# Four inverse square roots per token group: from ScalarE's Ln and Exp to a VectorE-only chain

## The reference

```
x = x + attention(layernorm(x));   x = x + fp8_gemm(bf16(layernorm(x)), kernel) + bias
layernorm(x) = (x - mean) / sqrt(var + 1e-5)
attention: q, k, v = x @ W.T, 16 heads of 16 features, each mapped by
    exp_map(v) = 1/sqrt(c) * tanh(sqrt(c) * |v|) * v/|v|
  dist = 1/sqrt(c) * arccosh(max(1 + 2c * |q-k|^2 / ((1 - c|q|^2)(1 - c|k|^2)), 1 + 1e-5))
  weights = softmax(-softplus(beta) * dist - bias)
  out = log_map(exp_map(weights @ log_map(exp_map(v)))) @ W_o.T
```

## Time and profile before

| what | us |
|---|---|
| median of 3 runs (2428.98 to 2432.98) | 2432.06 |
| the profiled execution's own time | 2433.24 |
| span of its trace | 2431.4 |
| ACT busy (80% of the span) | 1937.7 |
| PE busy (80%) | 1945.1 |
| DVE busy (40%) | 970.8 |
| POOL busy (15%) | 362.6 |
| mean granted TensorE clock, share of full | 0.809 |

### The profile page before, as it was taken

One profiled execution on the slowest core, in us unless ns is written; L12 is line 12 of the kernel. 1 busy time (PEld: TensorE's weight loads), 2 busy tenths in 40 slices (PEclk: granted clock), 3 DMA queues, 4 the chain that ended last, 5 costly groups with the idle time before them and its releaser, 6 DMA issues. The chain is left out here.

```text
span 2431.4 us, 29241 instructions
## 1 busy us (share of the span) xinstructions
PE 1945.1 (80%) x10317; PEld 624.6 (26%) x10317; DVE 970.8 (40%) x2289; ACT 1937.7 (80%) x1184; POOL 362.6 (15%) x223
## 2 busy tenths in 40 slices
PE   4458897989888768888879489798979888888682
PEld 2222232323222222222323123232323222222221
DVE  4432344343534345343444534443343534221413
ACT  1039999998989659998989389899988989999491
POOL 1111121121212002020212102121121212010011
PEclk9959798988888778897989579898888888876675
DMA  1120101001010200202020020201001010200000
GB/s 37 57 57 10 49 10 51 25 19 58 18 58 1 66 9 11 65 1 75 1 66 10 1 75 1 66 10 66 10 18 58 18 49 1 66 1 18 1 18 10
DMA packets 79154, 75.58 MB, mean 31 GB/s; under 512 B 34651, under 2 KB 60508, under 8 KB 78940
## 3 DMA queue, kind: packets, MB, share of 16 engines
q1 hardware_dynamic: 78940, 73.02, 9.6%
HBM read 17.96 MB, written 55.05 MB: 30 GB/s over the span
## 5 line engine op out<-in xcount | busy, mean ns | idle before, releaser
L911 ACT ACTIVATE U<-ps 128x2048 f32<-128x2048 f32 x500 | 939.0, 1878 | 178.6 <-PE ps L820 169.3
L916 ACT ACTIVATE U<-U,sc 128x2048 f32<-128x2048 f32 x512 | 1025.4, 2003 | 0.0
L820 PE MATMUL ps<-q_T,k_T 18*128 18x512 f32 x4096 | 750.4, 770 | 222.7 <-ACT U L911 149.2
L833 PE MATMUL ps<-U,vals 128*32 128x512 f32 x4096 | 680.6, 743 | 50.1 <-ACT U L916 29.1
L820 PEld LDWEIGHTS ps<-q_T,k_T 18*128 18x128 f32 x4096 | 224.5, 218 | 756.0 <-ACT U L911 592.5
L340 PE MATMUL ps<-wT,xnT 128*128 128x384 f32 x512 | 231.7, 581 | 13.7 <-DVE qkv L370 9.4
L370 DVE COPY qkv<-ps 128x384 f32<-128x384 f32 x128 | 71.4, 558 | 342.4 <-PE ps L340 334.8
L306 POOL TENSOR_TENSOR sqr<-qkv 128x768 f32<-128x768 f32 x64 | 94.1, 1470 | 732.4 <-DVE qkv L370 651.2
L833 PEld LDWEIGHTS ps<-U,vals 128*32 128x32 f32 x4096 | 87.9, 118 | 327.7 <-ACT U L916 216.6
L348 PE MATMUL ps<-ident,rows 128*128 128x128 f32 x512 | 99.2, 325 | 84.6 <-POOL rows L323 66.6
L340 PEld LDWEIGHTS ps<-wT,xnT 128*128 128x128 f32 x512 | 98.3, 213 | 161.5 <-issue 107.2
(11 more groups left out here) (174 smaller groups left out, 1336.3 us busy)
## 6 DMA issues: line engine op xcount, KB each, us to landing
q_scratch<-q_T SPq DMA_DIRECT2D x16, 1024.0 KB, 4.5
k_scratch<-k_T SPq DMA_DIRECT2D x16, 1024.0 KB, 6.9
v_scratch<-vals SPq DMA_DIRECT2D x16, 768.0 KB, 10.9
xt<-in_L_attn_x_dram SPq DMA_DIRECT2D x16, 512.0 KB, 3.8
fi_xt<-in_L_attn_x_dram SPq DMA_DIRECT2D x16, 512.0 KB, 4.7
out_dram<-fi_x SPq DMA_DIRECT2D x16, 512.0 KB, 3.2
rk_scratch<-rk SPq DMA_DIRECT2D x16, 32.0 KB, 12.2
wraw<-in_L_attn_W_q_dram SPq DMA_DIRECT2D x1, 256.0 KB, 2.9
```

Of the source, the lines that this page charges most:

```text
L820: ins = pe.matmul(g.ps[:, 2 * pair + i, :], a.k_T[HB * h:HB * h + RD, b % 2, hg, kt * P:(kt + 1) * P], a.q_T[HB * h:HB * h + RD, G % 3, hg ...
L833: ins = pe.matmul(g.ps[HB * h:HB * h + VW, 6, :], a.vals[:, b % 2, kt, (hg * HPG + h) // 2, DH * (h % 2):DH * (h % 2) + VW], U[:, n % RING ...
L911: act.activation(U[:, n % RING].rearrange("p b n -> p (b n)"), chunk(n), ACT.Ln, scale=-2.0 / EPS, bias=1.0).then_inc(ln_done, 1)
L916: act.activation(U[:, n % RING], U[:, n % RING], ACT.Exp, scale=g.NEGB).then_inc(exp_done, 1)
```

## The change

ACT's eight instructions per pair of stages (L407, L409, L412, L414, L616, L618, L621, L623) and their semaphores are gone, and `finish.scalar` with them. DVE makes each inverse square root alone, in the slot where it made its Newton step: one instruction that turns the number's bits into a first guess, and three Newton steps of three instructions, where there was one of four. The Newton step is written with `scalar_tensor_tensor`, which does two operations on two tensors in one instruction. The semaphore counts of the chains change with it (29 to 41 and 22 to 34 steps per group), and two small tiles fall away in each stage.

```diff
+SEED = 1597463007.0
+def inverse_root(v, step, x, y, t):
+    step(v.tensor_scalar(y.bitcast(I32), x.bitcast(I32), -0.5, SEED, ALU.mult, ALU.add))
+    for _ in range(3):
+        step(v.tensor_tensor(t, y, y, ALU.mult))
+        step(v.scalar_tensor_tensor(t, t, -0.5, x, ALU.mult, ALU.mult))
+        step(v.scalar_tensor_tensor(y, t, 1.5, y, ALU.add, ALU.mult))
...
-            act.wait_ge(ss_rdy, n + 1)
-            act.activation(lnss[:, :, :], ss[:, :, :], ACT.Ln).then_inc(a_steps, 1)
-            act.wait_ge(a_steps, 2 * n + 2)
-            act.activation(y[:, :, :], lnss[:, :, :], ACT.Exp, scale=-0.5).then_inc(y0_rdy, 1)
...
         if k == 20:
-            v.wait_ge(y0_rdy, n + 1)
             v.wait_ge(ss_rdy, n + 1)
-            step(v.tensor_tensor(y2[:, :, :], y[:, :, :], y[:, :, :], ALU.mult))
-            step(v.tensor_tensor(y2[:, :, :], y2[:, :, :], ss[:, :, :], ALU.mult))
-            step(v.tensor_scalar(y2[:, :, :], y2[:, :, :], -0.5, 1.5, ALU.mult, ALU.add))
-            step(v.tensor_tensor(y[:, :, :], y[:, :, :], y2[:, :, :], ALU.mult))
+            inverse_root(v, step, ss[:, :, :], y[:, :, :], y2[:, :, :])
             v.tensor_tensor(nrm[:, :, :], ssqk, yqk, ALU.mult).then_inc(n_rdy, 1)
```

More of the change, by code:

```diff
@@ L250, in sb @@
         return _sb(nc, ctx, name, shape, dt)
-    PER = 29
+    PER = 41
     xt = sb("xt", [P, GT, D])
     stats, mv = sb("stats", [P, GT, 6]), sb("mv", [P, GT, 2])
-    veps, lnv, rstd, rtmp = (sb(n, [P, GT]) for n in ("veps", "lnv", "rstd", "rtmp"))
+    veps, rstd, rtmp = (sb(n, [P, GT]) for n in ("veps", "rstd", "rtmp"))
     xnT = sb("xnT", [P, 2, GTOK])
@@ L265, in project_stage @@
     prod = sb("prod", [1, 3, H])
[L266 to L269, removed]
+    (x_in, var_rdy, xn_rdy, sq_rdy, red_done, ss_rdy, n_rdy, vg_rdy, e_rdy, small_rdy, rows_rdy, amax_rdy,
+     amax_r_rdy, d_steps, o_steps) = (_sem(nc, ctx, "pr_" + n) for n in (
+         "x_in", "var", "xn", "sq", "red_done", "ss", "n", "vg", "e", "small", "rows", "amax", "amax_r",
+         "v_steps", "open_steps"))
     v_rdy = _sem(nc, ctx, "pr_v_rdy")
-    steps_before = {0: 0, 2: 8, 20: 12, 22: 17}
+    steps_before = {0: 0, 2: 8, 20: 18, 22: 29}
     def start_vector(v):
@@ L431, in vector @@
         if k == 2:
-            v.wait_ge(rs0_rdy, n + 1)
             v.wait_ge(var_rdy, n + 1)
[L434 to L437, removed]
+            inverse_root(v, step, veps[:, :], rstd[:, :], rtmp[:, :])
             for t in range(GT):
@@ L490, in vector @@
             v.sem_inc(amax_rdy, 1)
-        assert step.n == {0: 8, 2: 4, 20: 5, 22: 12}.get(k, 0), (k, step.n)
+        assert step.n == {0: 8, 2: 10, 20: 11, 22: 12}.get(k, 0), (k, step.n)
     p = Shared()
@@ L511, in finish_stage @@
     stats, mv = sb("stats", [P, GT, 6]), sb("mv", [P, GT, 2])
-    veps, lnv, rstd, rtmp, rmax = (sb(n, [P, GT]) for n in ("veps", "lnv", "rstd", "rtmp", "rmax"))
+    veps, rstd, rtmp, rmax = (sb(n, [P, GT]) for n in ("veps", "rstd", "rtmp", "rmax"))
     xb, xq = sb("xb", [P, GT, D], BF16), sb("xq", [P, GT, D], BF16)
@@ L517, in finish_stage @@
         ocT[:, :, :].rearrange("p c n -> p (c n)")
[L518 to L522, removed]
+    (f_in, osq_rdy, oss_rdy, oy2_rdy, oc_rdy, var_rdy, sp_rdy, sum_rdy, xq_rdy, yb_rdy, yb2_rdy, res_rdy, res_out,
+     steps_v) = (_sem(nc, ctx, prefix + n) for n in (
+         "in", "osq", "oss", "oy2", "oc", "var", "sp", "sum", "xq", "yb", "yb2", "res", "out", "steps_v"))
     psb = g.ps[:, 7, :].bitcast(BF16)
-    steps_before = {5: 0, 7: 1, 13: 5, 15: 13, 17: 20}
+    steps_before = {5: 0, 7: 1, 13: 11, 15: 19, 17: 32}
     def sync(sp, n, k):
@@ L611, in copy @@
             v.sem_inc(yb_rdy, 1)
[L613 to L623, removed]
     def vector(v, n, k):
@@ L648, in vector @@
             v.wait_ge(var_rdy, n + 1)
-            v.wait_ge(rs0_rdy, n + 1)
-            step(v.tensor_tensor(rtmp[:, :], rstd[:, :], rstd[:, :], ALU.mult))
-            step(v.tensor_tensor(rtmp[:, :], rtmp[:, :], veps[:, :], ALU.mult))
-            step(v.tensor_scalar(rtmp[:, :], rtmp[:, :], -0.5, 1.5, ALU.mult, ALU.add))
-            step(v.tensor_tensor(rstd[:, :], rstd[:, :], rtmp[:, :], ALU.mult))
+            inverse_root(v, step, veps[:, :], rstd[:, :], rtmp[:, :])
             for t in range(GT):
@@ L923, in unit @@
                             power(n - 1)
-                        if G >= 1:
-                            finish.scalar(act, G - 1, s)
                         if G + 2 < NG:
@@ L943, in _ @@
                 power(N - 1)
-                for k in range(32):
-                    finish.scalar(act, LAST, k)
             @block.vector
@@ L1251, in _ @@
                 groups(pe, group)
-            @block.scalar
-            def _(act):
-                act.preload_act_table_set(ACT_SET)
-                def group(n):
-                    for k in range(32):
-                        finish.scalar(act, n, k)
-                groups(act, group)
             @block.vector
```

18 lines of the change are left out of this document (6 added, 12 removed).

## The result

The changed kernel is slower: 2444.75 us, the median of 17 runs (2432.51 to 2452.03), beside 2431.79 for the kernel before in the same measurement, a ratio of 1.0053 with a 95% interval from 1.0038 to 1.0067. The forecast was 2422. The profiled execution of it took 2443.74, with a span of 2441.9 against 2431.4.

A forecast was written before the change was run, and what follows sets the result against it. ACT and PE take turns as the bound, DVE matters only where one waits for it. Terms -16.4 - 9.3 + 15.3 - 5.5 - 0.8 - 3.0 + 5.0 + 1.5 + 2.5 = -10.7 gave 2422, range 2406 to 2441.

The forecast's parts named there:

- Slot 14/15: L621 and L623 delay their step by 0.79; the OTs copy comes 0.8 later, about 0.2 is left; 15 groups, -3.0.
- Slot 19/20: ACT loses 1.26 of delay, the longer DVE chain still ends with 1.6 to spare; 13 groups, -16.4.
- gain taken back: Rival at slot 19: longer DVE chain or late POOL work takes half or more of 16.4; 2430 and up; chance 0.18.
- Clock helps: Rival: less PE idle time in slot 20, so the clock may hold right after; -10, 2411; chance 0.19.
- Slots 1 to 5: ACT is free earlier, PE takes up its gap, -9.3; the chain makes x 1.2 later, 13 groups, +15.3.
- Slot 6: The logarithm no longer stands behind L616 and L618; about 0.42 a group saved, -5.5.
- Ahead of the loop: ACT's round trip goes and the whole chain is added, for `ss` and `rstd`; +5.0.
- behind: Behind the loop the chain is likewise on the path; +0.9 and +0.6, +1.5.
- group 8: Step 20 is open there and step 21's logarithm waits for DVE, with the longer chain in that path; +2.5.
- The clock rival: Slots 1 to 6: longer wait for x prolongs PE's half clock by a step, about 1.4; +18, 2440; chance 0.17.

The follow-up runs named there:

- wide fill: Changed kernel with two more PE products (128 rows, 512 moving columns) in slot 17, where PE waits for the OTs copy; 2422.69 us.
- slot 15 back: Changed kernel with the root of slots 14 and 15 given back to ACT and one Newton step, the other three on VectorE alone; 2406.56 us.
- slot 15 earlier: Changed kernel with the ten root instructions of slot 15 issued in slot 14, x minus mean times rstd staying in slot 15; 2401.10 us.
- six-step run: Kernel before with only the root of slots 19 and 20 on VectorE alone, and six Newton steps there in place of three; 2447.22 us.
- slot 20 root alone: Kernel before with only one of the four roots changed, that of slots 19 and 20 (q, k, v norms); 2394.88 us.

## Why the prediction was wrong

**The failing step is "Slot 14/15".** It said that the OTs copy comes 0.8 later and that of the 0.79 gained about 0.2 is left, -3.0 in all. Two errors are in it.

The first is the size of the delay. The 0.8 credits the old chain with 0.4 of waiting for ACT, and it had none: it began behind a copy of PE's product, with `rstd` there since 612.47. The kernel before, group 3:

```profile
612.27 0.20 ACT L623 ACTIVATE fi_rstd<-fi_lnv 128x4 f32<-128x4 f32 x1
...
617.05 0.56 DVE L370 COPY qkv<-ps 128x384 f32<-128x384 f32 x1 [3.51 <-PE ps L340]
617.53 0.15 DVE L650 TENSOR_TENSOR fi_rtmp<-fi_rstd 128x4 f32<-128x4 f32 x1
...
618.32 1.38 DVE L655 TENSOR_SCALAR fi_xb<-fi_x,fi_mv,fi_rstd 128x256 bf16<-128x256 f32 x4
...
622.48 0.56 DVE L370 COPY qkv<-ps 128x384 f32<-128x384 f32 x1 [0.53 <-DVEq L1050]
```

So the whole growth counts, 1.18 (1.97 for 0.79). Besides, the 0.77 that ACT gains at slot 14 moves its logarithms up by more than the product that the chain stands behind: the chain begins 5.41 behind the start of slot 15's logarithm in place of 5.15, in all eleven groups. That makes 1.44, near the step from 0.93 to 2.32 in the shortest waits. Within each kernel the wait takes two values, 0.3 apart. They go with VectorE's idle time at the branch ahead of the copies (DVEq), which is near 0.54 or near 0.86 in both kernels. The 0.2 doesn't follow from the prediction's own terms either: 0.79 less 0.8 is nothing. By itself the wait costs 0.97 a group (slot 18 with the wide fill, 4.62 against 3.65), half of the 0.77 and 1.26 gained beside it.

The large error is the second: no price was put on what PE's idle time does to its clock there. Half clock turned up in the prediction at X and at slot 20, where the trace before showed it, but not at slot 17, where the trace showed full clock beside a wait of 0.93 to 1.26. With the wait at 2.3 and more the fall came in 11 of 11 groups, and took 3.4 from each. The three runs that remove it (slot 15 back, slot 15 earlier, wide fill) land at 2407, 2401 and 2423, and six instructions that only delay the copy (2456) bring it about in the kernel before.

**"Slot 19/20", -16.4, was right as mechanism and size.** Alone it gives 1.27 a group (forecast 1.26), `nrm` comes in time, and the slack is the 1.6 that was read, as the six-step run shows. It paid nothing in the change because PE was the bound at half clock in slots 18 and 19. The rival "gain taken back" named the right place and the wrong cause: the nine instructions were 0.395 apart, and POOL did no harm.

**"Clock helps", the rival at 0.19,** did not come in the change, but it did in the kernels that leave the slot 17 wait short. With the slot 20 root alone slots 20 to 27 are 1.55 shorter, about as much as the forecast's own 1.26. So the forecast of 2422 was also too cautious about its own mechanism: with slot 15's root one slot earlier and all else as in the change, the time is 2401.

**"Slots 1 to 5"** held: -1.02 and +1.44 against -0.72 and +1.18 (13 x 1.2 is 15.6, not the 15.3 of the sum); the first guess stood 1.85 beside POOL, and PE's wait is 3.90 (forecast near 3.7). **Slot 6** gave 0.96 in place of 0.42, since ACT there no longer waits for PE at half clock either (the gap that the forecast read as 0.24 to 0.60 was 0.93 in group 2): the stretch that begins at slot 4.2 lasts 10.5 to 11 in all eleven groups; before it lasted 14 in five, and five had one of 24 from slot 1 on. With slot 2's root back on ACT it lasts 14 again in ten of them, and slot 6 takes 4.79. Why the longer wait for x goes with a shorter stretch is not shown. **Ahead of the loop** it was +1.7 for a forecast +5.0, **behind** +2.7 for +1.5, **group 8** +3.7 for +2.5; from 151 to 171 in the kernels here, the time ahead of the loop varies by more than the chains explain, and that stays open.

**The clock rival** (slower by the wait for x, 2440) had the kind of cause right and the place wrong: the stretch behind X got shorter, and giving slot 2 back to ACT left the falls at slot 18.

**Its size per event was also off**, 1.4 for one step; a fall at slot 18 costs 3.4 to 3.9, since it lasts two to three steps.

What stays open is why a group falls or holds at the same wait. At 0.92 to 1.28 it fell in 2 of 11 groups with slot 15 back, and in none of 11 in the kernel before and with the slot 20 root alone. In the kernel with slot 15 earlier the three short falls came in groups whose wait was 0.60 or 0.61, and none in those of 0.83 to 0.87. With 2.3 and more it fell every time, with 1.3 and less seldom; what decides in a single group isn't shown.
